# Starting the state recurrence four places earlier and giving it eleven places a step instead of twelve

## The reference, cut to what matters

```python
x = x + tanh(g_xattn) * ssm(ctx, layernorm(x))      # state-space block
x = x + tanh(g_ffn) * ffn(layernorm(x))             # shared expert + 7 routed experts, top 3
# ssm, per batch: u = silu(conv(in_proj(ctx))); delta = softplus(...)
def step(state, xs):                                # 512 time steps, 16 states per channel
    d_t, B_t, C_t, u_t = xs
    state = state * exp(d_t * A) + (d_t * u_t) * B_t
    return state, (state @ C_t)
# y = (sum over states + D*u) * silu(z)
# ffn: out = F(x; shared) + sum_e F(x; expert e) * w_e,  F(x) = (silu(x@W1) * (x@Wg)) @ W2
```

## Time and profile before

| | |
|---|---|
| median of 3 runs | 1487.75 us (1487.33 to 1488.89) |
| the profiled execution: its time, its span | 1491.74 us, 1489.9 us |
| busy PE / PE weight loads / DVE / ACT / POOL | 1401.8 / 1080.6 / 1053.2 / 512.3 / 430.7 us |
| mean granted TensorE clock | 0.968 of full speed |
| steps 2 to 5 of round 0 | 44.1 to 44.6 us each |
| steps 2 to 5 of rounds 1 and 2 | 40.0 to 40.3 us each |
| step 1 of rounds 0, 1, 2 | 34.3, 33.7, 33.6 us |
| a step of the last round, from step 3 | 32.6 us |

### The profile page before, as it was taken

The page is one execution under the profiler, slowest core; times in us unless marked ns, Lnnn a source line. Parts: engine busy times, 40 slices in busy tenths (PEclk is TensorE's granted clock), DMA queues, the critical chain, the costliest instruction groups (busy, mean ns, idle before and its releaser), DMA issues.

```text
span 1489.9 us, 18123 instructions
## 1 busy us (share of the span) xinstructions
PE 1401.8 (94%) x6290; PEld 1080.6 (73%) x6290; DVE 1053.2 (71%) x1271; ACT 512.3 (34%) x859; POOL 430.7 (29%) x224
## 2 busy tenths in 40 slices
PE   8778889999999989999999979999999999999999
PEld 4444466777777767777778857777777878888887
DVE  6788876898899874689999864689999853222222
ACT  4766635444433323433233123433233111111111
POOL 0000023678777711123232211123233211111111
PEclk8899989999999999999999989999999999999999
DMA  6234414756776664455555554455555554655552
GB/s 207 78 134 148 163 43 147 283 206 236 248 254 227 219 231 130 153 186 177 178 183 174 193 213 129 155 184 178 179 185 174 189 174 161 205 194 193 186 169 84
DMA packets 90797, 266.38 MB, mean 179 GB/s; under 512 B 11472, under 2 KB 11600, under 8 KB 90336
## 3 DMA queue, kind: packets, MB, share of 16 engines
q1 hardware_dynamic: 85472, 258.39, 51.4%
q10 hardware_dynamic: 5248, 6.96, 1.3%
HBM read 207.39 MB, written 57.93 MB: 178 GB/s over the span
## 4 chain that ended last, share of the span: by engine, by line
PE 70%; DVE 18%; issue 5%; ACT 5%; DMA 0%; POOL 0%; ACTq 0%; DVEq 0%; POOLq 0%
PE ps_hg L464 19%; PE ps_h L464 18%; PE ps_y L464 12%; PE ps_y L616 7%; DVE st L1148 7%; PE ps_mid L542 5%; DVE y_rows L1154 3%; PE ps_h L534 2%; ACT dA L807 2%; DVE st L1139 1%; DVE u L1028 1%; PE ps_mid L512 1%; DVE h_tmp L1274 1%; DVE h_tmp L1269 1%; PE ps_mid L508 1%
## 5 line engine op out<-in xcount | busy, mean ns | idle before, releaser
L1425 POOL TENSOR_TENSOR h_lo<-h_tmp,h_hi 128x512 fp32r<-128x512 f32 x128 | 281.1, 2196 | 780.2 <-ACT h_hi L879 780.2
L464 PE MATMUL ps_h<-x_hi,w_split 128*128 128x512 f32 x1024 | 352.7, 406 | 9.6 <-issue 5.3
L464 PE MATMUL ps_hg<-x_hi,wg_split 128*128 128x512 f32 x1024 | 351.3, 404 | 0.0
L1148 DVE TENSOR_TENSOR_SCAN st<-dA,st 128x1024 f32<-128x1024 f32 x128 | 296.6, 2328 | 0.0
L464 PE MATMUL ps_y<-w_split,h_hi 128*128 128x512 f32 x1024 | 256.5, 398 | 1.2 <-ACT h_hi L879 1.2
L464 PEld LDWEIGHTS ps_h<-x_hi,w_split 128*128 128x128 f32 x1024 | 196.2, 192 | 52.0 <-issue 7.5
L879 ACT ACTIVATE h_hi<-h_tmp 128x512 fp32r<-128x512 f32 x128 | 81.0, 632 | 433.2 <-DVE h_tmp L1274 433.2
L464 PEld LDWEIGHTS ps_hg<-x_hi,wg_split 128*128 128x128 f32 x1024 | 196.9, 192 | 41.4 <-issue 0.2
L1269 DVE SCALAR_TENSOR_TENSOR h_tmp<-h_tmp,ps_h 128x512 f32<-128x512 f32 x128 | 87.8, 686 | 185.7 <-ACT h_tmp L873 185.3
L464 PEld LDWEIGHTS ps_y<-w_split,h_hi 128*128 128x128 f32 x1024 | 189.0, 189 | 40.0 <-ACT h_hi L879 2.4
L464 PE MATMUL ps_hg<-x_lo,wg_split 128*128 128x512 f32 x512 | 203.0, 396 | 0.0
(11 more groups left out here) (140 smaller groups left out, 1120.5 us busy)
## 6 DMA issues: line engine op xcount, KB each, us to landing
w_split<-split_scratch SPq DMA_DIRECT2D x192, 512.0 KB, 4.9
wg_split<-split_scratch SPq DMA_DIRECT2D x96, 512.0 KB, 4.3
split_scratch<-w_split SPq DMA_DIRECT2D x64, 512.0 KB, 4.2
b_all<-xd_scratch SPq DMA_DIRECT2D x64, 256.0 KB, 3.9
split_scratch<-wg_split SPq DMA_DIRECT2D x32, 512.0 KB, 3.1
w_raw<-in_W_dram SPq DMA_DIRECT2D x14, 1024.0 KB, 7.9
wg_raw<-in_Wg_dram SPq DMA_DIRECT2D x7, 1024.0 KB, 10.0
dA<-in_x_dram SPq DMA_DIRECT2D x4, 1024.0 KB, 7.6
```

Source lines behind the costliest of these rows:

```text
L464: mm = pe.matmul(out_, lhs[a], rhs[c], start=first and q == 0, stop=last and q == len(sides) - 1)
L1148: dve.tensor_tensor_scan(flat[1], flat[0], flat[1], 0.0, ALU.mult, ALU.add).then_inc(scan_done, 1)
L1425: pool.tensor_tensor(h_lo[:, j, :], h_tmp[j % 2][:], h_hi[:, j, :].bitcast(F32), ALU.subtract).then_inc(hl_ready, 1)
```

## The change

States begin at place 4 of step 1, so that state 0 and state 1 lie there whole (eight slots). Steps 2 to 5 have eleven slots (none at place 11), step 6 twelve, step 7 five as before. The slots are numbered in one table; 64 precede step 7 in both kernels. Since eleven is no multiple of four, a state begins at places 0, 4, 8 in step 2; 1, 5, 9 in step 3; 2, 6, 10 in step 4; 3, 7 in step 5; 0, 4, 8 in step 6. PE's transposes, the decays and the loads of B follow the table. In step 1 DVE's `front_z2` of tiles 0 and 1 goes from place 3 to place 0, router part 1 from place 5 to place 3, `front_z2` of tiles 2 and 3 and a memset from place 7 to place 4, all ahead of the slot of that place; ACT's `front_z` of tiles 0 and 1 goes into the end of the shared step (ahead of the weight splits for `w2` there), that of tiles 2 and 3 from j = 2 to j = 1; the decays of step 1 are 2, 2, 4, 4 in place of 0, 2, 2, 4; PE's z transposes go to g = 2 and 3. In round 0 SP's fetch of raw w1 and wg comes behind all the B loads of the step instead of ahead of the last one.

```diff
+        PLACES = 2 * T + 4
+        SLOTS = [(1, p) for p in range(T, PLACES)]
+        for e in range(2, NE):
+            SLOTS += [(e, p) for p in range(PLACES if e == NE - 1 else PLACES - 1)]
+        SLOTS += [(NE, p) for p in range(T + 1)]
+        def slot_of(e, p):
+            return divmod(SLOTS.index((e, p)), T) if (e, p) in SLOTS else (DS, T)
+        LOADS = {2: {1: (4,), 3: (5, 6)}, 3: {2: (7,), 3: (8,)}, 4: {0: (9,), 2: (10,), 3: (11,)},
+                 5: {1: (12,), 3: (13, 14)}, 6: {1: (15,)}}
+        DECAYS = [(0, 2), (2, 4), (4, 8), (8, 12)]
+        for e in range(2, NE):
+            for j in range(T):
+                d = DECAYS[-1][1]
+                DECAYS.append((d, min(T * DS, d + (2 if j == T - 1 else 3))))
...
# SP, round 0
-            store_up(2)
+            store_up(2, (0, 1, 2))
+            load_b(1, 2)
+            store_up(2, (3,))
             load_up(3, 2)
-            load_b(1, 2)
+            load_b(1, 3)
             for e in range(2, NE):
-                n = 3 * (e - 2) + RING + 1
                 store_down(e)
                 load_down(e + 1, e)
-                store_up(e + 1, (0, 1))
-                load_b(1, n)
-                store_up(e + 1, (2, 3))
-                if n + 1 < DS:
-                    load_b(1, n + 1)
+                for j in range(T):
+                    store_up(e + 1, (j,))
+                    for n in LOADS[e].get(j, ()):
+                        load_b(1, n)
                 if e + 1 < NE:
                     load_up(e + 2, e + 1)
-                if n + 2 < DS:
-                    load_b(1, n + 2)
...
# PE
+                    if e == 1 and g in (2, 3):
+                        front(m, f"z{g}")
+                    n, i = slot_of(e, g)
+                    if n < DS + 1 and n > 0 and i < T:
+                        state_to_rows(m, n - 1, i)
...
# ACT
                         front_ln(m, range(T))
+                        front_z(m, (0, 1))
...
                     if j == 0:
                         router_exp(b)
-                        front_z(m, (0, 1))
                     if j == 1:
-                        decays(m, 0, 2)
-                    if j == 2:
                         front_z(m, (2, 3))
-                        decays(m, 2, T)
-                    if j == 3:
-                        decays(m, T, 2 * T)
+                    decays(m, *DECAYS[j])
...
# DVE
                 def first_routed(p):
+                    if p == 0:
+                        front_z2(m, (0, 1))
                     if p == 1:
                         router(b, 0)
                     if p == 3:
-                        front_z2(m, (0, 1))
-                    if p == 5:
                         router(b, 1)
-                    if p == 7:
+                    if p == 4:
                         front_z2(m, (2, 3))
                         front_zero(m, 1)
-                    if p >= 2 * T:
-                        slot(m, 0, p % T)
+                    place(1, p)
...
-                    step_(STEPS * b + e, e - 1, lambda p: slot(m, 3 * (e - 2) + 1 + p // T, p % T))
+                    step_(STEPS * b + e, e - 1, lambda p: place(e, p))
```

More of the change, by code:

```diff
@@ L224, in gated_block @@
         block = ctx.enter_context(nc.Block())
+        PLACES = 2 * T + 4
[3 more added lines that the diff above has]
+        SLOTS += [(NE, p) for p in range(T + 1)]
+        assert SLOTS.index((NE, 0)) == T * DS
+        def slot_of(e, p):
[7 more added lines that the diff above has]
+                DECAYS.append((d, min(T * DS, d + (2 if j == T - 1 else 3))))
         def conv_in(m, et):
@@ L429, in _ @@
                 fetch_down(b, 1)
-                fetch_up(b, 2)
+                fetch_up(b, 2, (0, 1, 2))
                 load_b(m, 2)
+                fetch_up(b, 2, (3,))
+                load_b(m, 3)
                 fetch_down(b, 2)
                 for e in range(2, NE):
-                    n = 3 * (e - 2) + RING + 1
-                    fetch_up(b, e + 1, (0, 1))
-                    load_b(m, n)
-                    fetch_up(b, e + 1, (2, 3))
-                    if n + 1 < DS:
-                        load_b(m, n + 1)
-                    if n + 2 < DS:
-                        load_b(m, n + 2)
+                    for j in range(T):
+                        fetch_up(b, e + 1, (j,))
+                        for n in LOADS[e].get(j, ()):
+                            load_b(m, n)
                     fetch_down(b, e + 1)
@@ L653, in shared_step, with state_sums @@
                 step_(STEPS * b, between)
-            def state_sums(m, first):
+            def state_sums(m, e):
                 def between(g):
-                    n = first + g // T
-                    if 0 <= n < DS:
-                        state_to_rows(m, n, g % T)
+                    if e == 1 and g in (2, 3):
[3 more added lines that the diff above has]
+                        state_to_rows(m, n - 1, i)
                 return between
@@ L664, in batch @@
                 shared_step(b, m)
-                step_(STEPS * b + 1, lambda g: front(m, *{4: ("z2",), 5: ("z3",)}.get(g, ())))
-                for e in range(2, NE):
-                    step_(STEPS * b + e, state_sums(m, 3 * (e - 2)))
-                step_(STEPS * b + NE, state_sums(m, DS - 1))
+                for e in range(1, NE + 1):
+                    step_(STEPS * b + e, state_sums(m, e))
                 x2_to_columns(m)
@@ L955, in batch @@
                 for e in range(2, NE):
-                    ahead = T * (3 * (e - 2) + 2)
-                    routed_step(STEPS * b + e, lambda j: decays(m, ahead + 3 * j, ahead + 3 * (j + 1)))
+                    routed_step(STEPS * b + e, lambda j: decays(m, *DECAYS[T * (e - 1) + j]))
                 routed_step(STEPS * b + NE, lambda j: front_conv(m + 1) if j == T - 1 and m + 1 < NB else None)
@@ L1361, in shared, with place @@
                         front_du(m)
+                def place(e, p):
+                    n, r = slot_of(e, p)
+                    if r < T:
+                        slot(m, n, r)
                 def first_routed(p):
+                    if p == 0:
+                        front_z2(m, (0, 1))
                     if p == 1:
@@ L1366, in first_routed @@
                     if p == 3:
-                        front_z2(m, (0, 1))
-                    if p == 5:
                         router(b, 1)
-                    if p == 7:
+                    if p == 4:
                         front_z2(m, (2, 3))
                         front_zero(m, 1)
-                    if p >= 2 * T:
-                        slot(m, 0, p % T)
+                    place(1, p)
                 def last(p):
-                    slot(m, DS + p // T, p % T) if p <= T else None
+                    place(NE, p)
                     if p == T:
```

## The result

The changed kernel takes 1518.63 us (median of 4, 1515.86 to 1522.14) against 1488.32 us: ratio 1.0205, 95% interval 1.0181 to 1.0229, so 30.3 us slower. Its profiled execution took 1517.43 us with a span of 1515.6. That is 25.7 above the profiled execution before, mainly because the latter, with 1491.74, was 3.4 above its kernel's median. The four executions of the changed kernel lie 6 us apart; the executions before in this study, profiled one included, lie 4 us apart (1487.33 to 1491.74).

The account below looks back on a forecast made before the run. PE was taken to bound every step, so only its waits count: 14.2 us (rounds 1 and 2) + 10 (step 1, round 0) - 2.6 (steps 2 to 6, round 0) = 21.6, added to 1487.75: 1509.4 us, range 1488 to 1524.

Parts of the forecast that it names:

- likeliest case: Whole kernel: even scans and a full step 1 cost as forecast, 1509 us, holding from about 1500 to 1518; chance 0.60.
- chain of 4.35 us: Even places: end of up(j), tanh, L1269, sum, scan, PE take 4.35 us; PE arrives after 3.2 and waits 1.14.
- Transposes and PE as the bound: PE bounds every step; four transpose groups join step 1, one leaves each of steps 2 to 5: 2.1 us each way, cancelling.
- Even scans in rounds 1 and 2: Steps 2 to 6: PE waits longer for scans on even places, 3.9 us a round, bounds nothing to 6.
- Step 1 in rounds 1 and 2: PE waits 1.0, 1.5 and 0.75 us, sum 3.2 a round where there was no wait; bounds nothing to 5.
- wait of 1.0 in gate(3): Step 1, rounds 1 and 2: PE waits 1.0 us for L1274 of j = 2; on time would show the prediction wrong.
- Step 1 of round 0: The same chain, worse: 7.5 us of added waits and 2.5 of slow stretches, together 10 us; bounds 3 and 15.
- Steps 2 to 6 of round 0: Relief of 7.8 us against even scans 3.4 and late raw weights 1.8: sum -2.6 us, bounds -16 and +5.
- The relief: Round 0, steps 3 to 6: POOL's splits end sooner, 1.1 us won in each, two slow stretches gone: -7.8 us.
- The slow clock spreads: Rival: waits in step 1 and pairs in steps 3 and 5 bring PE to 1.2 GHz; 1523 us or more, chance 0.12.
- Relief pays fully: Rival: steps 3 to 6 of round 0 fall from 44.6 to 40.0, -18.4 us; chance 0.10 below 1484.8, 0.13 for 1490 to 1500.
- It only moves work: Rival: same matmuls and transposes, waits traded for waits, 1488 us; needs 10.4 us more DVE work in step 1; chance 0.05.

Follow-up runs that it names:

- e8: The changed kernel with ACT's decays of steps 2 to 6 behind the tanh of up(j), three fewer made in step 1: 1497.96 us.
- e7: The changed kernel with two decays behind j = 2 of step 1 and six behind j = 3, in place of four and four: 1517.33 us.
- e12: The changed kernel with the ranking in router part 1 replaced by four tiny memsets, so the output is another: 1515.74 us.
- e2: The changed kernel with router part 1 back at place 5 of step 1: 1530.83 us.
- e1: The changed kernel with raw w1 and wg fetched ahead of the load of B that waits for a late multiply: 1517.29 us.
- e3: The changed kernel with 12, 10, 12, 10, 12 places in steps 2 to 6, every scan on an odd place, raw weights fetched early: 1497.38 us.
- e4: The kernel before with its table shifted by one place, states from place 7 of step 1, every scan on an even place: 1552.11 us.
- e5: The changed kernel, early start kept, with 12, 12, 12, 12, 8 places in steps 2 to 6, every scan on an odd place: 1501.84 us.
- e10: The changed kernel with the places of e3 and the decays behind the tanh as in e8: 1483.79 us.
- e11: The kernel before with decays behind the tanh (1475.10 us), and POOL's h_lo moved ahead of its two weight splits: 1469.31 us.

## Why the prediction held, and where it did not

The sign and the places held, and several of the sizes: forecast 1509.4 us in a range of 1488 to 1524, measured 1518.6, which is just outside the 1500 to 1518 of the likeliest case. The sum was +21.6; the difference of the medians is +30.3, that of the profiled executions +25.7. The terms are compared below on the profiled executions. (Two readings in the prediction are loose, and nothing hangs on them: of the chain of 4.35 us the 0.67 and the 0.14 do not stand in the earlier trace rows, and 378.1 + 7.9 is 386.0, not 386.5.)

**Transposes and PE as the bound: right.** Four groups more in step 1 and one fewer in steps 2 to 5; step 2 of rounds 1 and 2 fell by 0.4 us, against 0.52 forecast, and PE's busy time is 1404.4 us against 1401.8.

**Even scans in rounds 1 and 2: right in kind, too small.** The chain of 4.35 us gave a wait of 1.14, measured 1.13. But I let each even wait stand alone and named the drag only as the upper bound. Measured: step 3 +1.9 to +2.0 and step 5 +2.1 to +3.7, where 1.9 and 1.4 less 0.5 for the transposes were forecast. Steps 2 to 6 together came to +4.5 and +3.2 a round, against +1.8. The missing term is ACT's queue (e8): rounding, then three decays, then the tanh, 0.72 us on three of the four waits of steps 3 and 5. The 1.6 us between the two rounds are one slow stretch; and step 4 did not have the 0.6 us that I gave it. The rows that would have shown it are ACT's timeline of the kernel before, where the tanh of up(3) already came late (step 3 of round 2):

```profile
1042.19 0.72 ACT L807 ACTIVATE dA<-delta,neg_A 128x511 f32<-128x511 f32 x1 [1.06 <-DVE st L1148]
1042.82 0.58 ACT L873 ACTIVATE h_tmp<-ps_h 128x512 f32<-128x512 f32 x1
```

Its product was followed by PE's transposes at 1041.49, so it is 1.1 us late, behind a decay that waited for a scan. I had put 0.67 us from the end of up(j) to L1269 for all j.

**Step 1 in rounds 1 and 2: right in sum, partly by luck.** Forecast 3.2 us of waits and 2.1 of transposes; with the shared step it measured +5.5 and +4.3. The waits came to 1.4 us, not 3.2, and in round 1 a slow stretch of 1.6 us in the shared step (clock 0.97), which I had not forecast, fills the gap. Step 1 itself is 36.3 and 36.2 us, where I wanted 38 to 39. The wait of 1.0 in gate(3) did not come: L1284 of j = 2 was on time in these two rounds, which the prediction had named as a sign of being wrong. The first multiply took 1.22 us there and not the 2.00 of the earlier trace rows: that duration belonged to its old place, beside POOL, not to the memset. POOL in round 1 before, then DVE in round 1 after:

```profile
634.53 1.30 POOL L1425 TENSOR_TENSOR h_lo<-h_tmp,h_hi 128x512 fp32r<-128x512 f32 x1 [4.56 <-ACT h_hi L879]
...
639.18 1.22 DVE L1149 TENSOR_TENSOR st<-u,b_all 128x1024 f32<-128x1024 f32 x1
```

The waits for `h_hi` (0.98 against 1.5) and for the scan (0.42 against 0.75) are there. e7 shows that four decays ahead of the tanh make the first of them.

**Step 1 of round 0: right in place, a little too large.** Waits of 4.30, 0.93 and 0.34 against 4.8, 2.0 and 0.75; with the shared step +9.7 us, forecast 10 + 2.1. Step 1 alone is 41.1 us, not the "over 43" of the prediction. e12 and e2 show that it is the line of router, z and multiply, and that the router is not all of it.

**Steps 2 to 6 of round 0: the step that failed.** Forecast -2.6 and -2.1 for the transposes, measured +3.0. Its parts: the raw weights cost nothing (e1), where I had 1.8. The relief is real: step 6, whose table is unchanged, fell from 43.3 to 40.7, step 4 from 44.6 to 41.6. What failed is "the even scans (3.9 as above)": in round 0, where ACT has two weight splits in each j and POOL collides with DVE, the second even wait is 3.3 us and brings a slow stretch of its own. Steps 3 and 5 lost 3.3 and 5.3 us, while I gave them the price of the later rounds and the relief on top. Against e3, which has them on odd places and a slot less, they are 10.8 us longer; about 1 of that is the two groups of transposes that e3 lacks there. So the term that I put at 3.4 measures near 10. Together it is +8.6 in steps 3 and 5 and -5.6 in steps 4 and 6. This part was missed by 7.7 us, more than the whole was in the profiled executions (25.7 less 21.6: 4.1); step 1 of round 0 and the scatter ahead of the rounds, 2.4 each the other way, hid some of it.

**The rivals.** "The slow clock spreads" is partly what happened: in rounds 1 and 2 a stretch at 1.2 GHz came in one step 5 of two in the profiled execution, and in each of steps 2 to 5 of e4. "Relief pays fully" was half right, in the steps with odd scans; the even ones ate it. "It only moves work" is refuted by e3 and e5, which move as much and lose 9 and 13 us.

"It would need step 1 to hold 10.4 us more DVE work": DVE's busy time in step 1 of round 2 is 32.41 us against 23.97 in round 1 before, 8.4 more.

Where the 21 us between the changed kernel and e3 went is shown: some 14 are the even scans alone (e10 against e8), some 7 what ACT's queue adds to them. The remaining 9 us are a balance. The shared step and step 1 together cost 18 us over the rounds in e5, in which steps 2 to 5 are those of the kernel before, and the steps behind them give half of it back in e3. Which share of the 18 each queued operation has is only bounded by e2, e7 and e12. The last order of POOL on the early start was not tried.

## What to carry to other kernels

Before moving work into a place between two stages, write down for each engine what stands between the event that ends one PE product and the operation that PE waits for; a place counts by what is queued ahead of it, not by the idle time of the engine over the step. When pieces of unequal length alternate (a scan of 2.28 us, a multiply of 1.22), put the long one into the interval that has the shorter chain ahead of it. Here that is the odd place, behind gate(j), where PE waited 0.57 us; at the even place, behind up(j), tanh and L1269, it waited 1.13 and more. A table whose pieces change parity changes every wait. Work that has no deadline in a step (the decays) belongs into the interval in which its engine waits for another one, not between two links of the chain; that edit alone made the unchanged kernel 1.0% faster, and the order of one POOL operation 0.4% more.

## What the runs showed of the hardware

The granted clock fell to 1.2 GHz after waits shorter than the 2.14 us that the trace of before had shown: two waits of 1.85 us, 15 to 16.5 us apart, went with a mean clock of 0.96 in the steps of e4, while pairs of 1.14 us in e8 left 1.00. In the changed kernel two waits of 1.85 us brought a slow stretch in one step 5 and not in another of the same execution (43.7 and 42.1 us). Behind the first of the two waits in round 1, then in round 2:

```profile
794.30:798.30 4.00, 4.00 (x14) 3.23 (x15) 2.23 (x3) 2.47 (x4) 2.18 (x1) 0.62 0.49 165
...
1137.00:1141.00 4.00, 3.86 (x21) 3.32 (x22) 2.38 (x4) 2.90 (x5) 2.20 (x1) 1.00 0.48 172
```

That such stretches make the scatter of the changed kernel is likely and not shown step by step: its slowest execution (1522.14 us) has a mean clock of 0.964, its fastest (1515.86) 0.968.

A wait of one engine for another can hide a transfer entirely: 3.2 us of waiting for raw weights cost nothing (e1).

Whether a POOL operation was under way at its start decided how long a DVE operation on two SBUF operands took. In the changed kernel's timelines 85 scans started without one and took 2.26 to 2.28 us, 15 with one and took 2.71 to 3.37; the multiplies took 1.21 to 1.22 (71) and 1.46 to 2.33 (25). The other way round, POOL's `h_lo` took 1.3 us at its shortest, and 2.5 to 3.3 where a scan was under way at its start. The Trainium skill (SBUF — State Buffer, Who interferes with whom) says that the one that comes first keeps the shared port for its whole instruction. e11 agrees as far as DVE goes: with POOL's split gone from that moment the scan at place 1 is 2.28 us.
